# Exponentials and masks of two neighbouring dense tiles in one operation each, over PSUM banks in the order 0, 1, 2, 1

## The reference, cut to what matters

```python
sim = einsum('pbnhd,pkhd->pbnhk', q, pk_keys)        # 2 x 64 key scores per token and head
scores, idx = top_k(sim, 16)
score = scores[0][..., :, None] + scores[1][..., None, :]   # 16 x 16 sums
final_scores, pk_idx = top_k(score, 16)              # the best 16 of 64 x 64 pairs
final_scores = softmax(final_scores)
k = einsum('bnhk,bnhkd->bnhd', final_scores, keys_table[ind])
v = einsum('bnhk,bnhkd->bnhd', final_scores, values_table[ind])
```

## Time and profile before

| | us |
|---|---|
| median of 3 runs | 3269.15 |
| lowest and highest run | 3267.7, 3270.88 |
| span of the profiled execution | 3918.3 |
| the profiled execution's own time beside its span | not given |
| granted TensorE clock in it, mean | 0.862 |
| PE, PEld, DVE, ACT, POOL busy | 3008.9, 1391.1, 2785.8, 2039.4, 2057.7 |
| dense tiles, from the first to the last score | 353 to 3710 |

### The profile page before, as it was taken

How to read it: one execution, slowest core, us unless ns; L and a number is a source line. 1 busy time by engine, 2 the same in 40 slices (tenths; PEclk the granted TensorE clock), 3 DMA queues, 4 the chain that set the end, 5 groups by cost and what they waited for, 6 DMA issues and landing times.

```text
span 3918.3 us, 39268 instructions
## 1 busy us (share of the span) xinstructions
PE 3008.9 (77%) x9722; PEld 1391.1 (36%) x9722; DVE 2785.8 (71%) x9999; ACT 2039.4 (52%) x4498; POOL 2057.7 (53%) x2095
## 2 busy tenths in 40 slices
PE   4861657878787878878778868888778878888888
PEld 2430223333333333333333433333333433333343
DVE  7678777777777777776777887777768786874433
ACT  3231545555555555655555655556555655555532
POOL 3011666666656665555565655556656655655400
PEclk8985777888787888989888989888888988989899
DMA  1001121212121111112121212111111212121100
GB/s 37 22 8 52 44 66 43 62 45 57 48 56 47 52 52 50 52 46 55 44 59 38 65 40 57 44 52 53 51 50 46 57 46 56 42 62 39 33 3 3
DMA packets 85626, 179.86 MB, mean 46 GB/s; under 512 B 40177, under 2 KB 41107, under 8 KB 85398
## 3 DMA queue, kind: packets, MB, share of 16 engines
q0 software_dynamic: 66560, 135.40, 13.1%
q1 hardware_dynamic: 18838, 41.94, 3.5%
HBM read 176.15 MB, written 1.05 MB: 45 GB/s over the span
## 4 chain that ended last, share of the span: by engine, by line
PE 41%; DVE 25%; another core or an unknown queue 11%; issue 8%; ACT 8%; ACTq 0%; DVEq 0%
PE mx_acc L1430 12%; PE mx_O L1442 7%; PE mx_area L1476 6%; DVE mx_W L1787 5%; PE mx_D L1420 4%; ACT mx_GT L1691 3%; DVE mx_KVs L2013 3%; PE mx_area L1456 2%; ACT mx_W L1623 2%; DVE mx_mx_part L2031 2%; PE mx_area L1492 1%; DVE mx_mx L2031 1%; PE mx_X L1560 1%; PE mx_area L1486 1%
## 5 line engine op out<-in xcount | busy, mean ns | idle before, releaser
L1402 POOL DMA_INDIRECT mx_G<-in_kv_table,mx_slot_i x2048 | 2004.0, 978 | 1394.6 <-issue 590.1
L1430 PE MATMUL mx_acc<-mx_W,mx_table 128*128 128x512 f32 x2048 | 1180.7, 660 | 1.6 <-ACT mx_kvT L1630 0.7
L1787 DVE SCALAR_TENSOR_TENSOR mx_W<-mx_D,mx_W 128x512 f32<-128x512 f32 x1024 | 699.1, 683 | 297.5 <-ACT mx_W L1623 180.5
L1623 ACT ACTIVATE mx_W<-mx_D 128x512 f32<-128x512 f32 x1024 | 606.6, 593 | 523.2 <-PE mx_D L1420 231.0
L1691 ACT ACTIVATE mx_GT<-mx_G,mx_slot_w 128x128 f32<-128x128 f32 x2048 | 759.2, 495 | 3.2 <-DVE mx_KVs L2013 1.1
L1420 PE MATMUL mx_D<-mx_U,mx_pick_b 96*128 96x512 bf16 x1024 | 432.7, 423 | 110.8 <-DVE mx_W L1787 52.5
L1430 PEld LDWEIGHTS mx_acc<-mx_W,mx_table 128*128 128x128 f32 x2048 | 436.1, 214 | 201.9 <-issue 104.5
L1647 ACT ACTIVATE mx_PT<-mx_area 128x512 f32<-128x512 f32 x472 | 241.8, 514 | 464.9 <-PE mx_area L1480 146.3
L1442 PE MATMUL mx_O<-mx_PT,mx_KVs 128*65 128x512 f32 (+3 forms) x768 | 347.5, 536 | 170.0 <-ACT mx_PT L1647 82.8
L1456 PE MATMUL mx_area<-mx_KTa,mx_QTa 64*128 64x512 f32 (+3 forms) x384 | 200.6, 607 | 132.6 <-DVE mx_mx L2031 66.1
L2013 DVE TENSOR_REDUCE mx_KVs<-mx_GT 128x128 f32<-128x2048 f32 x128 | 291.9, 2280 | 6.0 <-ACT mx_GT L1691 5.9
(11 more groups left out here) (390 smaller groups left out, 4462.4 us busy)
## 6 DMA issues: line engine op xcount, KB each, us to landing
mx_table<-in_kv_dense SPq DMA_DIRECT2D x64, 512.0 KB
mx_G<-in_kv_table,mx_slot_i POOLq DMA_INDIRECT x2048
tz_table<-in_c_dft SPq DMA_DIRECT2D x1, 2048.0 KB
tz_table<-in_c_idft SPq DMA_DIRECT2D x8, 256.0 KB, 2.6
out_h<-mx_xc SPq DMA_DIRECT2D x4, 256.0 KB
mx_G<-in_c_pick SPq DMA_DIRECT2D x1, 528.0 KB
st_h<-in_tok_W,em_ids POOLq DMA_INDIRECT x32
st_keys<-in_pk_keys SPq DMA_DIRECT2D x1, 512.0 KB, 3.9
```

The source lines that it names most:

```text
L1402: pool.indirect_dma_start(G[g % RING][:, r, :], None, a["kv_table"], bass.IndirectOffsetOnAxis(slot_i[n % 2][:, k, r:r + 1], 0))\
L1430: pe.matmul(acc[:, :], table[:, tile, :], W[c % TILE_RING][:, :], start=(tile == 0), stop=(tile == TILES - 1)).then_inc(applied, 1)
L1623: act.activation(W[c % TILE_RING][:, :], D_ps[c % 3][:, :], ACT.Exp).then_inc(p_done, 1)
L1787: dve.scalar_tensor_tensor(W[c % TILE_RING][:, :], D_ps[c % 3][:, :], 0.0, W[c % TILE_RING][:, :], ALU.is_ge, ALU.mult).then_inc(w_done, 1)
```

## The change

Tiles c (even) and c+1 become a pair. Both lie in neighbouring banks, and one ACT instruction and one DVE instruction of 1024 columns replace two of 512. The order of banks is 0, 1, 2, 1: the pairs use banks 0 and 1, then 1 and 2, and the odd tile is always in bank 1. W becomes one tensor of 6 slots, with the two tiles of every second pair swapped to match. Both instructions are issued in the position of the odd tile. `corner_of` follows the banks, with 4 fresh tiles per half instead of 6, and the host lays the dense table out in the same order. The semaphores p_done and w_done rise by 2. POOL's transfers wait in groups of four.

```diff
+BANK_OF = (0, 1, 2, 1)
@@ def corner_of(tile):
-    bank, step = tile % 3, tile // 3
-    pair, eighth = (bank, step) if step < 8 else (3, 3 * bank + step - 8)
-    return pair // 2, pair % 2, eighth, step in (0, 8)
+    if tile % 2:
+        pair, eighth = 2 + tile // 16, tile // 2 % 8
+    else:
+        pair, eighth = tile // 2 % 2, tile // 4
+    return pair // 2, pair % 2, eighth, eighth == 0
@@ def mixer_stage
-        W = [m.sb(f"W{i}", [P, HALF]) for i in range(TILE_RING)]
+        W_ring = m.sb("W", [P, TILE_RING, HALF])
-        D_ps = [m.ps(f"D{i}", [P, HALF]) for i in range(3)]
+        D_banks = m.ps("D", [P, 3, HALF])
+        D_ps = [D_banks[:, i, :] for i in range(3)]
+        def D_of(c):
+            return D_banks[:, BANK_OF[c % 4], :]
+
+        def W_of(c):
+            first = c // 2 * 2 % TILE_RING
+            return W_ring[:, first + (c + c // 2) % 2, :]
+
+        def pair_of_banks(c):
+            lower = c // 2 % 2
+            return D_banks[:, lower:lower + 2, :]
+
+        def pair_of_W(c):
+            first = c // 2 * 2 % TILE_RING
+            return W_ring[:, first:first + 2, :]
@@ gpsimd
-                    ahead = SLOT * n + 8 * k - 6 + r // 2
-                    if r % 2 == 0 and ahead > 0:
+                    ahead = SLOT * n + 8 * k - 6 + r // 4 * 2
+                    if r % 4 == 0 and ahead > 0:
                         pool.wait_ge(w_done, ahead)
@@ def score_dense(c):
-                if c >= 3:
-                    pe.wait_ge(w_done, c - 2)
+                if c >= 4:
+                    pe.wait_ge(w_done, c - 1 if c % 2 else c - 2)
+                elif c == 3:
+                    pe.wait_ge(w_done, 2)
                 if fresh:
-                    pe.matmul(D_ps[c % 3][:, :], pick_b[:, 0, :], U[n % 2][:, 2 + jh, cols], start=True, stop=False,
+                    pe.matmul(D_of(c), pick_b[:, 0, :], U[n % 2][:, 2 + jh, cols], start=True, stop=False,
                               skip_group_check=True)
-                step = 1 + eighth // 3 if fresh else 3 + eighth
-                pe.matmul(D_ps[c % 3][:, :], pick_b[:, step, :], U[n % 2][:, ih, cols],
+                step = 1 if fresh else 3 + eighth
+                pe.matmul(D_of(c), pick_b[:, step, :], U[n % 2][:, ih, cols],
@@ def apply_dense(c):
-                pe.matmul(acc[:, :], table[:, tile, :], W[c % TILE_RING][:, :], start=(tile == 0),
+                pe.matmul(acc[:, :], table[:, tile, :], W_of(c), start=(tile == 0),
@@ scalar
-            def exp_dense(c):
+            def exp_pair(c):
...
-                act.activation(W[c % TILE_RING][:, :], D_ps[c % 3][:, :], ACT.Exp).then_inc(p_done, 1)
+                act.activation(pair_of_W(c), pair_of_banks(c), ACT.Exp).then_inc(p_done, 2)
...
-                if 0 <= c + 3 < PAIRS * SLOT:
-                    exp_dense(c + 3)
+                if 0 <= c + 3 < PAIRS * SLOT and c % 2 == 0:
+                    exp_pair(c + 3)
@@ vector
-            def mask_dense(c):
+            def mask_pair(c):
                 dve.wait_ge(p_done, c + 1)
-                dve.scalar_tensor_tensor(W[c % TILE_RING][:, :], D_ps[c % 3][:, :], 0.0, W[c % TILE_RING][:, :],
-                                         ALU.is_ge, ALU.mult).then_inc(w_done, 1)
+                dve.scalar_tensor_tensor(pair_of_W(c), pair_of_banks(c), 0.0, pair_of_W(c),
+                                         ALU.is_ge, ALU.mult).then_inc(w_done, 2)
...
-                    if 0 <= c + 3 < PAIRS * SLOT and not masked:
-                        mask_dense(c + 3)
+                    if 0 <= c + 3 < PAIRS * SLOT and c % 2 == 0 and not masked:
+                        mask_pair(c + 3)
```

## The result

| | before | after |
|---|---|---|
| median, us | 3268.43 | 3311.62 |
| lowest and highest of 4 runs | 3266.13, 3270.88 | 3309.2, 3315.45 |
| ratio after to before, 95% interval | | 1.0124 [1.011, 1.0139] |
| span of the profiled execution, us | 3267.6 | 3309.8 |
| mean granted TensorE clock | 0.922 | 0.936 |

The kernel became slower by 43 us. The profiled execution of after took 3311.85 us, 2 us more than its span.

A forecast was written before the change was run, and what follows sets the result against it. It took PE and DVE to bound the kernel in alternating regimes within every slot, no engine near full. Terms -15 - 4 - 6 + 14 = -11 us took 3269 to 3258 us, with an 8-in-10 range of 3208 to 3312.

The forecast's parts named there:

- Durations: Wide operations on DVE and ACT: a double mask would last about 1220 ns, a double exponential about 1020 ns.
- the chained rows: DVE runs where a mask of 683 ns adds only 0.59 or 0.60 us; taken to show 0.06 us saved per pair.
- Masks -15: DVE: 512 double masks replace 1024, saving 15 us on the path, ends 0 and 75.
- exponentials -4 us: ACT: paired exponentials save 4 us on the path, ends 0 and 31.
- Fresh starts -6: PE, line 1417: 64 fewer matmuls that start a bank afresh save 6 us, ends 0 and 14.
- The wait at the score +14: PE: odd scores wait for a nearer, wider mask; one loss per slot, 16 x 0.9 = 14 us, ends 0 and 127.
- Gathers 0: POOL: the last four gathers released up to 0.97 us later, covered by ACT reading five positions on; cost 0.
- What the change lets wait: Step on PE, DVE and ACT waits from the shorter distance at even positions and wider operations, costing 14 us.
- the slower rival: PE's wait for the mask at odd scores decides, 0.97 us per passage: 3308 us with half the passages, 3371 with all; chance 0.33.
- Its forecast of its own sign: The slower rival would show PE's waits for DVE masks at the score grown to over 200 us.
- the range of 8 in 10: Whole kernel: from 3208 us, leaving out deeper full credit, up to 3312 us, holding half of the passages.

The follow-up runs named there:

- before_fill_first: Kernel before, with masks behind the maxima and PE filling the area banks ahead of the position's score and application: 3281.39 us, ratio 1.0043.
- the second profile: Kernel before, unedited, profiled again because its first profile was disturbed: the profiled execution took 3269.59 us, span 3267.6 us.
- single_0121: Kernel before with banks 0, 1, 2, 1 and 64 fewer fresh starts, but single operations and gathers in twos: 3276.19 us, ratio 1.0025.
- before_odd_waits: Kernel before, with only an odd tile's score waiting for the mask two tiles back instead of three: 3274.31 us, ratio 1.0021.
- the disturbed execution: First profiled execution of the kernel before, unedited, which the prediction used: span 3918.3 us, with 11% of it on an unknown queue.
- the two runs on the gathers: Changed kernel with gathers released four masks earlier: 3309.57 us, ratio 1.0131; kernel before with gathers released in fours: 3269.67 us, ratio 1.0012.
- pair_counts: Changed kernel with p_done and w_done counting pairs (increment 1, thresholds halved): 3298.64 us, ratio 1.0105.
- exp_single_mask_pair: Changed kernel with two exponentials of 512, each in its own position, and the wide mask kept: 3286.48 us, ratio 1.0057.

## Why the prediction was wrong

It said 3258 us, faster at 0.50; the result is 3311.62, on the slower side (0.33) and just inside the upper end of 3312. Step by step:

- **Durations: right.** 1219 and 1020 ns for 1220 and 1020. The wide mask occupies DVE for 1.14 us (1630.62 to 1631.76), as worked out. The Trainium skill (VectorE: DVE Perf Modes, section on the TRN2 errata) states a fixed cost of 120 cycles at 0.96 GHz per PSUM-source instruction, from which an estimate of 125 ns per pair follows. The trace agrees by duration: a pair saves 2 x 681 - 1219 = 143 ns. But DVE's busy time fell by 16 us, 31 ns per pair, so on the engine most of it had been hidden already, as the chained rows said.
- **Masks -15, exponentials -4 us: not seen on the path.** DVE's 16 us and ACT's 27 us of busy time went. The one stretch that got shorter without an explanation of its own is that from position 55, 1.0 us per slot; before_fill_first, which pairs nothing, has 20.5 us there too. So a shorter stretch there needs no pairing, and a catching up of what was late earlier in the slot is the likelier reading. The share of the path was sized too large as well: masks are 6% of the chain of the second profile, 196 us, still a third of them and not "perhaps a half".
- **Fresh starts -6: seen in one place, not in the sum.** The stretch from position 47 lost 0.6 us in every kernel with the new banks, single_0121 among them: 10 us over 16 slots. That kernel as a whole is 10 us slower than before, though, and the distance explains 7; so whether the 10 us reach the end is open.
- **The wait at the score +14: half of that for the distance.** before_odd_waits puts it at 7 us. The part with the wider operations, in positions 39 to 46, was not measured alone.
- **Gathers 0: the number holds within 0 to 8 us, its reason doesn't.** "its line 1691 sat idle 3.2 us in all" and "the cover is there" were read from the disturbed execution. The second profile of before has this (times, longest behind it):

```profile
ACT mx_GT L1691 <- DMA mx_G<-in_kv_table,mx_slot_i: 215.3, 60, 10.6
```

  ACT waits 215 us for gathers, and POOL's gathers are 8% of the chain. There was no such cover. Only the two runs on the gathers show that releasing them in fours explains at most a small part of the 43 us.
- **The step that failed** is "What the change lets wait". It listed what stands behind the waiting score on PE, and ended there: "behind those ACT's line 1647 and DVE's maxima". It never asked what stands on DVE behind the wider mask itself. There the maxima are next in line, and behind them PE's next fill. So the 0.43 + 0.54 us, worked out rightly, were charged to the wait at the score, where PE had room (in positions 32 to 38 the mask that it needs had ended 2.9 to 3.4 us earlier), and not to the loop from fill over maxima to the next fill, where it had none. The argument "in the maxima stretches PE is held closer to DVE by the area banks than by the masks" was counted against the slower rival. It was the mechanism: what lengthened DVE's order ahead of the maxima by 1.0 us at position 32 lengthened positions 31 to 38 by 2.6 us per slot.
- **The slower rival** had the right sign and size (3308) for a reason that the runs bear out for the smaller part only. Its forecast of its own sign, PE's waits at the score over 200 us, came true (288.1) and proves nothing, since the same wait at 244.7 us cost 7 us and at 338.2 us stood in an execution 33 us faster than that of after. The stretch that it wanted longer (16.7 to 17.9 us from position 39) did get longer, and there its reason fits the waits. That the result lies just inside the range of 8 in 10 is luck: the range's upper end was priced by passages over the score, not by the maxima.

The 43 us, as far as runs separate them: 29 by the place of the mask ahead of the maxima (in part the same time: 10 by the hand-over of an increment of two, 23 by the exponential's width), 7 by the distance (10 for the new banks as a whole, with fewer fresh starts), 0 to 8 by the gathers in fours. Each part is known to 5 to 7 us, and the parts overlap, since each was taken away alone; the sum is not exact.

## What to carry to other kernels

Merging two operations saved 143 ns of duration per pair here, and only 31 ns of DVE's busy time, and delayed everything queued behind the pair by the width of the second operation; before merging, list what comes next on the same engine, who waits for that, and whether that engine is full there (here PE, at 21.11 of 21.81 us). Work that another engine waits for is better put ahead of a wide operation whose consumer is positions away; here that gave back 29 us. The longest wait of a profile need not be the costliest one: test it by lengthening it alone, and look where in a slot it grew.

## What the runs showed of the hardware that was not expected

**A semaphore increment of two is not free.** In after, a mask that finds DVE idle starts 0.10 or 0.11 us after the exponential's end, in 109 of 112 cases between 1000 and 2600 us, and about 0.45 us after it in the 3 others; in before and in pair_counts it is 0.03 us in all 111 and 113 cases. exp_single_mask_pair, where only the mask still increments by two, has 0.10 or 0.11 us too (93 of 94 cases), so it is the waiting instruction's own increment that matters. In the trace's record such an instruction carries no wait of its own; a separate semaphore event ahead of it does the waiting. On ACT the same shows in the waits: after puts 177.1 us of the exponential's idle time down to "issue" and 28.8 to PE, pair_counts 198.7 to PE, as before did (184.6). In all it was 10 us (4 to 17).

**The granted clock rose while the time rose**, from 0.922 to 0.936. In the stretches shown it is 1.00 in both, so it explains none of the loss.
